# Expert layer of a two-layer decoder: inner values made transposed, gates repeated over the partitions through DRAM

## The reference

```
    def _L1_ffn_ref(x, W1, b1, W2, b2, Wr, br):
...
        logits = xf @ Wr + br
        _, topk_idx = jax.lax.top_k(logits, K)
        mask = jnp.zeros_like(logits).at[jnp.arange(T)[:, None], topk_idx].set(1.0)
        gates = mask + logits - jax.lax.stop_gradient(logits)
        h = jax.nn.relu(jnp.einsum('td,edh->eth', xf, W1) + b1[:, None, :])
        combined = jnp.einsum('te,eth,ehd->td', gates, h, W2) + gates @ b2
        return x + combined.reshape(B, S, D)
...
    x = x + _L1_ffn_ref(_layernorm(x, axis=-1), L1_ffn_W1, L1_ffn_b1, L1_ffn_W2, L1_ffn_b2, L1_ffn_Wr, L1_ffn_br)
```

## Time and profile before

| | us |
|---|---|
| median of three runs | 4103.48 (4102.7 to 4106.04) |
| profiled execution, its span | 4103.4 |
| PE busy | 3856.4 (94%) |
| DVE busy | 3013.6 (73%) |
| ACT busy | 2823.1 (69%) |
| POOL busy | 1820.6 (44%) |
| stage `experts`, first to last instruction on VectorE | 3744.09 to 4100.55 |

### The profile page before, as it was taken

One profiled execution on the slowest core, in us unless ns is written; L12 is line 12 of the kernel. 1 busy time (PEld: TensorE's weight loads), 2 busy tenths in 40 slices (PEclk: granted clock), 3 DMA queues, 4 the chain that ended last, 5 costly groups with the idle time before them and its releaser, 6 DMA issues. The chain is left out here.

```text
span 4103.4 us, 106549 instructions
## 1 busy us (share of the span) xinstructions
PE 3856.4 (94%) x33992; PEld 2993.1 (73%) x33992; DVE 3013.6 (73%) x7587; ACT 2823.1 (69%) x6420; POOL 1820.6 (44%) x1728
## 2 busy tenths in 40 slices
PE   7888899999979999898999989999999989998999
PEld 5666688888746666685666677888888867776777
DVE  7888655555569999657999955777777767775665
ACT  5666455555569999757999975777777767774333
POOL 3333222222258888536777753333333321112443
PEclk9999999999999999999999999999999989999999
DMA  0000100000010000100000010000000000000000
GB/s 18 9 9 10 48 8 6 6 6 6 7 43 9 8 8 8 27 18 10 8 8 8 13 28 29 1 0 0 0 0 0 0 3 4 3 3 6 12 12 12
DMA packets 109259, 42.48 MB, mean 10 GB/s; under 512 B 91232, under 2 KB 107872, under 8 KB 108512
## 3 DMA queue, kind: packets, MB, share of 16 engines
q1 hardware_dynamic: 109152, 41.10, 3.9%
HBM read 20.16 MB, written 4.19 MB: 6 GB/s over the span
## 5 line engine op out<-in xcount | busy, mean ns | idle before, releaser
L1142 POOL TENSOR_TENSOR l_rc<-l_rc,l_rs 128x1024 f32<-128x1024 f32 x128 | 303.6, 2372 | 201.4 <-DVE l_rs L1334 201.4
L1209 ACT ACTIVATE l_prob<-l_prob,l_mx 128x128 f32<-128x128 f32 x1024 | 312.1, 390 | 0.0
L1820 POOL TENSOR_TENSOR mb_steps<-w_upto,mb_dta 128x1024 f32<-128x1024 f32 x64 | 121.4, 1896 | 354.7 <-DVE mb_dta L2077 354.7
L711 POOL TENSOR_TENSOR ca_prob<-ca_prob,ca_sm 128x1232 f32<-128x1232 f32 x64 | 143.9, 2249 | 299.3 <-DVE ca_sm L877 299.3
L1234 PE MATMUL l_qk_ps<-w_local,l_hT 128*128 128x512 f32 x512 | 248.8, 609 | 13.1 <-DVE l_rs L1334 11.1
L1136 POOL TENSOR_TENSOR l_prob<-l_prob,l_sm 128x1024 f32<-128x1024 f32 x128 | 242.8, 1897 | 16.9 <-DVE l_sm L1320 16.9
L1119 POOL TENSOR_TENSOR l_rc<-l_rc,l_ss 128x1024 f32<-128x1024 f32 x128 | 243.4, 1902 | 12.5 <-POOL l_rc L1142 4.5
L1977 PE MATMUL mb_x_ps<-w_wx,mb_xT 128*128 128x256 f32 x1024 | 236.9, 384 | 0.0
L1329 DVE TENSOR_REDUCE l_ss<-l_sq 128x16 f32<-128x1024 f32 x128 | 156.1, 1219 | 77.3 <-ACT l_sq L1173 76.9
L2542 POOL TENSOR_TENSOR mo_hid<-mo_hid,mo_gate 128x1024 f32<-128x1024 f32 x64 | 121.7, 1901 | 201.7 <-DVE mo_hid L2688 201.7
L1977 PEld LDWEIGHTS mb_x_ps<-w_wx,mb_xT 128*128 128x128 f32 x1024 | 190.0, 191 | 23.2
(11 more groups left out here) (354 smaller groups left out, 11993.2 us busy)
## 6 DMA issues: line engine op xcount, KB each, us to landing
la_xin<-in_x SPq DMA_DIRECT2D x64, 64.0 KB
l_h<-lt_y SPq DMA_DIRECT2D x128, 32.0 KB
lt_quad<-lt_y SPq DMA_DIRECT2D x32, 128.0 KB
out_x<-k_x SPq DMA_DIRECT2D x64, 64.0 KB, 1.5
l_h<-lt_y SPq DMA_DIRECT2D x128, 31.8 KB
lt_quad<-lt_y SPq DMA_DIRECT2D x32, 127.0 KB
ca_ctxT<-in_ctx_T SPq DMA_DIRECT2D x128, 19.2 KB
wr_state<-in_p_state SPq DMA_DIRECT2D x1, 2438.5 KB, 11.9
```

The lines of the kernel that those rows point to most:

```text
L1142: gp.tensor_tensor(wide(rc[l][:]), wide(rc[l][:]), wide(rs[l][:]), ALU.add).then_inc(*pool_sum.did("rot"))
L1209: ex = sc.activation(p[:, a, j], p[:, a, j], ACT.Exp, bias=mx[l][:, a, j:j + 1])
```

## The change

The inner values are made with the inner index on the partitions, not the tokens. `w1` is held and `xnT` moves: eight products of 128 columns, piece j with the inner values of the experts 2j and 2j+1, partitions 0 to 63 the first and 64 to 127 the second. The eight turns of `hid` go. The bias now is one column for each piece (`b1`, 8 columns for 1024), so ScalarE adds it and applies the relu as it takes the values out of PSUM, in eight instructions of 128 columns; VectorE's add goes. `hid_ps` now has two lanes, `hidT` and `gateT` have four buffers.

The gates must then be repeated over the partitions. ScalarE's turned gates `gateT` (16 rows of 128) are stored by SP to `parked` in DRAM; SP waits for the landing and loads them back twice, the even experts' rows for partitions 0 to 63, the odd ones' for 64 to 127, each row read for 64 partitions, into `spread`. POOL multiplies `hidT` by `spread`. The bias product with `b2` moves behind the eight others. There are six parts, `NORM, TURN, ROUTE, GATE, SPREAD, OUT`: POOL multiplies batch n-4, PE's second product takes batch n-5, and VectorE's add and SP's store are for that batch too. The loop body has four steps.

```diff
-    "experts": (("w1", 1024), ("w2", 1024), ("b2", 128), ("wr", 16), ("b1", 1024), ("br", 16)),
+    "experts": (("w1", 1024), ("w2", 1024), ("b2", 128), ("wr", 16), ("b1", 8), ("br", 16)),
...
-        w1 = part["w1"].rearrange("p (e h) -> p e h", e=E)
+        w1 = part["w1"].rearrange("p (j n) -> p j n", j=CH)
...
+        hidT = [m.sb(f"hidT{i}", [128, CH, T]) for i in range(4)]
+        gateT = [m.sb(f"gateT{i}", [E, T]) for i in range(4)]
+        spread = both(m, "spread", [128, CH, T])
+        hid_ps = m.ps("hid_ps", [128, 2, CH, T])
...
             @block.sync
             def _(sp):
                 def step(at):
-                    b = at(LAST)
+                    b = at(GATE)
+                    if b:
+                        sp.wait_ge(*act_gate.at("gT", b))
+                        sp.dma_start(g.parked[b.lane], gateT[b.slot][:]).then_inc(parked[b.lane], 16)
+                        sp.wait_ge(parked[b.lane], b.loaded())
+                        for a in (0, 1):
+                            src = g.parked[b.lane].rearrange("(j a) t -> a j t", a=2)[a].partition_broadcast(64)
+                            sp.dma_start(spread[b.lane][64 * a:64 * a + 64], src).then_inc(spread_in[b.lane], 16)
+                    b = at(OUT)
                     if b:
...
             @block.gpsimd
...
-                    b = at(ROUTE)
-                    if b:
-                        l = b.lane
-                        gp.wait_ge(*vec_hid.at("hb", b))
-                        gp.tensor_tensor(hid[l][:], hid[l][:], gate[l][:].unsqueeze(2).to_broadcast([T, E, HID]), ALU.mult
-                                         ).then_inc(*pool_hid.did("hid"))
+                    b = at(SPREAD)
+                    if b:
+                        hid = hidT[b.slot][:]
+                        gp.wait_ge(*act_hid.at("h1", b))
+                        gp.wait_ge(spread_in[b.lane], b.loaded(32))
+                        gp.tensor_tensor(hid, hid, spread[b.lane][:], ALU.mult).then_inc(*pool_hid.did("hid"))
...
             @block.scalar
...
+                    b = at(TURN)
+                    if b:
+                        sc.wait_ge(*pe_turn.at("xnT", b))
+                        sc.wait_ge(*pe_route.at("h1", b, ago=2))
+                        sc.activation(xnT[b.lane][:], xn_ps[:, 0:T], ACT.Copy).then_inc(*act_turn.did("xnT"))
+                    b = at(GATE)
+                    if b:
+                        sc.wait_ge(*pe_gate.at("gT", b))
+                        sc.wait_ge(*pe_out.at("y", b, ago=4))
+                        sc.wait_ge(*pool_hid.at("hid", b, ago=2))
+                        sc.activation(gateT[b.slot][:], gate_ps[0:E, 0:T], ACT.Copy).then_inc(*act_gate.did("gT"))
                     b = at(NORM)
...
+                    b = at(ROUTE)
+                    if b:
                         for u in (0, 1):
-                            sc.wait_ge(*pe_out.at(f"hT{u}", b))
-                            sc.activation(hidT[l][:, 4 * u:4 * u + 4].rearrange("p j t -> p (j t)"),
-                                          turn_ps[:, 4 * u:4 * u + 4].rearrange("p j t -> p (j t)"), ACT.Relu
-                                          ).then_inc(*act_out.did(f"hT{u}"))
-                    b = at(TURN)
-                    if b:
-                        sc.wait_ge(*pe_turn.at("xnT", b))
-                        sc.activation(xnT[b.lane][:], xn_ps[:, 0:T], ACT.Copy).then_inc(*act_turn.did("xnT"))
-                pipeline(sc, g.NB, LAST + 1, step)
+                            sc.wait_ge(*pe_route.at(f"h{u}", b))
+                            sc.wait_ge(*pe_out.at("y", b, ago=4))
+                            for j in range(4 * u, 4 * u + 4):
+                                ex = sc.activation(hidT[b.slot][:, j], hid_ps[:, b.lane, j], ACT.Relu, bias=b1[:, j:j + 1])
+                            ex.then_inc(*act_hid.did(f"h{u}"))
...
             @block.tensor
...
-                    b = at(OUT)
-                    if b:
-                        l = b.lane
-                        te.wait_ge(*vec_route.at("gate", b))
-                        te.wait_ge(*act_out.at("hT1", b, ago=1))
-                        te.transpose(gate_ps[0:E, 0:T], gate[l][:], g.ident[:]).then_inc(*pe_out.did("gT"))
...
+                    b = at(GATE)
+                    if b:
+                        te.wait_ge(*vec_route.at("gate", b))
+                        te.wait_ge(*act_gate.at("gT", b, ago=1))
+                        te.transpose(gate_ps[0:E, 0:T], gate[b.lane][:], g.ident[:]).then_inc(*pe_gate.did("gT"))
+                    b = at(OUT)
+                    if b:
+                        te.wait_ge(*pool_hid.at("hid", b))
+                        te.wait_ge(*vec_out.at("x", b, ago=1))
+                        for j in range(CH):
+                            te.matmul(y_ps[:, 0:C], hidT[b.slot][:, j], w2[:, j], start=(j == 0), stop=False)
+                        te.matmul(y_ps[:, 0:C], gateT[b.slot][:], b2, start=False, stop=True).then_inc(*pe_out.did("y"))
...
-                        te.wait_ge(*vec_hid.at("hb", b, ago=1))
-                        for a in (0, 1):
-                            mm = te.matmul(hid_ps[:, a], xnT[l][:], w1[:, 8 * a:8 * a + 8].rearrange("p e h -> p (e h)"),
-                                           start=True, stop=True)
-                        mm.then_inc(*pe_route.did("h"))
-                    b = at(OUT)
-                    if b:
-                        l = b.lane
-                        te.wait_ge(*pool_hid.at("hid", b))
+                        te.wait_ge(*act_hid.at("h1", b, ago=2))
                         for u in (0, 1):
                             for j in range(4 * u, 4 * u + 4):
-                                mm = te.transpose(turn_ps[:, j], hid[l][:, 2 * j:2 * j + 2].rearrange("p e h -> p (e h)"),
-                                                  g.ident[:])
-                            mm.then_inc(*pe_out.did(f"hT{u}"))
-                        te.wait_ge(*act_out.at("gT", b))
-                        te.wait_ge(*vec_out.at("x", b, ago=1))
-                        te.matmul(y_ps[:, 0:C], gateT[l][:], b2, start=True, stop=False)
-                        for j in range(CH):
-                            if j % 4 == 0:
-                                te.wait_ge(*act_out.at(f"hT{j // 4}", b))
-                            mm = te.matmul(y_ps[:, 0:C], hidT[l][:, j], w2[:, j], start=False, stop=(j == CH - 1))
-                        mm.then_inc(*pe_out.did("y"))
-
-                pipeline(te, g.NB, LAST + 1, step)
+                                mm = te.matmul(hid_ps[:, l, j], w1[:, j], xnT[l][:], start=True, stop=True)
+                            mm.then_inc(*pe_route.did(f"h{u}"))
...
             @block.vector
...
-                        v.wait_ge(*vec_route.at("gate", b))
-                        v.wait_ge(*pe_route.at("h", b))
-                        v.wait_ge(*pe_out.at("hT1", b, ago=2))
-                        v.tensor_tensor(hid[l][:].rearrange("p e h -> p (e h)"), hid_ps[:].rearrange("p a n -> p (a n)"), b1,
-                                        ALU.add).then_inc(*vec_hid.did("hb"))
...
+    dram["parked"] = nc.dram_tensor("parked", [2, 16, T], F32, kind="Internal").ap()
```

42 lines of the change are left out of this document (20 added, 22 removed).

## The result

| | before | after |
|---|---|---|
| median (lowest to highest), us | 4103.73 (4102.58 to 4107.67) | 4115.85 (4114.2 to 4118.42) |
| ratio, 95% interval | | 1.0029 (1.0020 to 1.0038) |
| span of the profiled execution | 4103.4 | 4114.0 |

The change makes the kernel slower by 0.3%; I had forecast 1.0% faster. The steady steps gained nothing: between VectorE's 11th and 57th add to the stream a batch takes 5.43 us in both kernels. What is lost stands at the stage's ends. The first add is at 3763.98 instead of 3760.19 us, the ten steps behind it take 4.0 us more, the last seven 2.7 more, and the last add is at 4110.81 instead of 4100.26.

What follows compares the result with a forecast made beforehand. PE was taken to bound the `experts` stage, its step falling from 5.43 to 4.72 us. Start 3747.8 + fill 15 + 60 x 4.72 = 283.2 + drain 13.1 + end 2.85 gave 4062 us, range 4050 to 4096.

Steps and rivals of the forecast that it cites:

- PE's own step: PE's work per batch in the last stage, `experts`: falls from 5.43 to 4.72 us, saving 0.71.
- ScalarE: Eight evacuations with bias take 2.44 us, at most 3.08; ScalarE's 3.5 to 4.1 a batch is no bound by itself.
- VectorE: VectorE loses its add over 1024 values; it waits for PE anyway, so nothing is gained directly.
- Rival C: Gates reach PE's gate turn late: no stall or 0.1 us a batch, 4062 to 4068; within the main forecast's 0.60.
- The trip: Gates' way on SP's queue: store to DRAM, landing, two loads of 512 KB in all, POOL's wake; 4.6 to 5.3 us.
- D: Length of the gates' trip, from ScalarE's gate copy to POOL's wake: 4.6 to 5.3 us.
- packets much more than 27 ns: Sign named for being wrong first: the loads' 512-byte packets taking much longer than the 27 ns assumed.
- Round (1): Loop over three steps through PE, ScalarE, the trip and POOL: 13.3 to 14.0 us, hidden within 14.16.
- Rival A: Trip only half hides through slower data, landing or evacuations: step 4.85 to 5.3 us, 4070 to 4097; chance 0.20.
- Rival B: SP's queue sets the step: at the small load's 109 GB/s, step 6.7 us, time 4181; chance 0.13.
- round (2): SP's queue in order, loads' data, output store, next gate store, landing, wake: 3.6 to 4.3 us, under PE's 4.72.
- Sum: Forecast total time of the changed kernel: 4062 us, 41 us or 1.0% faster.

Runs made afterwards that it cites:

- e8: Changed kernel without POOL's product, the store of the gates and both loads; PE waits for ScalarE's evacuations instead: 4074.45 us, ratio 0.9932.
- e1: Changed kernel with VectorE's copy of the two largest values replaced by a reduction over an axis of one: 4104.06 us, ratio 1.0003.
- e5: Changed kernel with POOL's product reading one column of `spread` repeated instead of all of it: 4107.42 us, ratio 1.0012.
- e3: Changed kernel with loads reading an input's rows and waiting for POOL alone; store kept behind them, with SP's wait for it: 4126.74 us, ratio 1.0061.
- e14: e12 with PE's turn of `xn` also moved behind the second product, and ScalarE's copy of it: 4085.19 us, ratio 0.9957.
- e12: e6 with PE's gate turn behind the second product and ScalarE's gate copy behind its logarithm and exponential: 4083.81 us, ratio 0.9950.
- e13: Changed kernel with loads reading an input's rows and waiting for POOL alone, and no store of the gates: 4087.46 us, ratio 0.9963.
- e6: Changed kernel with one more step between gates and product (product n-5, second product n-6, four `spread` buffers): 4085.41 us, ratio 0.9952.

## Why the prediction was wrong

**PE's own step: right.** 4.72 forecast, 4.68 measured in e8. That is close in part by luck: the first product takes 1.87 in place of 1.98 and the second 1.94, while the gap behind the routing product is 0.1 wider.

**ScalarE: right, and cheaper.** Eight evacuations in a row start 0.25 us apart (383 ns each, overlapping), 2.2 us for all, against my 2.44.

**VectorE: the step that failed.** "It waits for PE anyway; nothing is gained directly" is true of the add that goes, and I stopped there. I looked at what VectorE waits for by semaphore, and at no other tie. In the kernel before POOL's product began right behind the gates of its own batch and VectorE's add, and was over before the next batch's copy: 0.17 us, 50 copies of 50. The change frees it from that place: when it runs is set by the trip. Nothing in the earlier trace rows shows the price of a copy beside a product, and the prediction does not name this as an unmeasured thing. The round that it closes costs 5.43 - 5.02 = 0.41 us a batch, 60 x 0.41 = 25 us. Taking the copy alone out of it gave 0.18 back (e1), since `xn` waits in its place.

**Rival C was true and too cheap.** I had 1.99 + 0.05 us from routing to the gates; e8 shows 2.40. The logits start 0.43 behind the start of routing (0.26 forecast), and L2689 takes 0.35 instead of 0.17. It reads two tiles of SBUF while POOL adds `xn` to the stream, and ends 0.03 us behind that add 50 times of 50: one more tie of VectorE to POOL. Coming late costs 0.3 a batch, some 18 us, against the 0 to 6 forecast.

**The trip: every term in its place, three too small.** D = 0.02 + 1.35 + 4.72 = 6.1 us, against 4.6 to 5.3. The store's part, 1.36, and the first byte of the loads, 1.35, were met. The data took 2.6 (1.7 to 2.4 forecast), the landing with wake 0.7 (0.35). The sign "packets much more than 27 ns" did not come: in the burst from 3888.5 to 3891.5 us the 1152 packets of 512 bytes take 27 ns in the median, 31 in the mean. The product took 2.35, the price of L1142 which I had named as the dear end and not taken; the full second operand costs what it costs there, as e5's 1.91 confirms.

The estimate from the Trainium skill ("DMA: Bandwidth & Descriptors", Anatomy of one DMA), 5.7 us, was nearer to D than my sum, but by luck. The store's part took 1.36 us and not 2.0, the loads' part 4.72 and not the 3.7 that 2.0 + 1.7 gives. The page has that figure for DMAs that GpSimd issues, and that it speaks against two dependent transfers was my conclusion from the figure. The Trainium skill ("SBUF — State Buffer", Door 1: The DMA port swizzle) gave an estimate of 2.4 us for the data, close to the 2.6 measured with `out_x` among them. Its 218 GB/s as a cap is less sure: in the two slices before the second load's first bytes, issued 0.63 us behind the first, 238 and 303 GB/s are shown, too short a stretch to decide.

**Round (1): "it hides" failed too, but did not set the time.** With the measured evacuations, product and trip it is 8.7 - 0.3 + 0.45 + 6.1 = 15.0, over the 14.16 of three steps. That is 5.0 a step, no more than PE takes in e8 anyway. The round that bound goes over two, with nothing but the gates, the trip and the product in it. It is closed by a link that is in no semaphore.

**Rival A** (PE idle through a trip that half hides) gave the size of the trip's excess but named POOL as the engine that PE waits for; PE waited for VectorE. **Rival B** did not come in the changed kernel, but round (2) did in e3 and e14, and SP was as full in e12. It came not through bytes: a small store behind a large load, waited for in order.

**Sum.** 4062 + 18 (gates late) + 25 (the copy's round) = 4105. The remaining 11 stand in filling and draining, by the adds shown at the top. e13 and e6, with the steady step of e8, carry 5 to 7 over 4062 + 18. How the rest is shared between the longer trip, the lower clock from 3760 on and copies that wait in the first steps was not separated.

## What to carry to other kernels

When an engine's work is moved to another time, ask what it will stand beside, not only whom it waits for. Here a GpSimd operation of 2.35 us held a VectorE copy, a `tensor_scalar` or an SBUF-only `tensor_tensor` until it ended, even a copy of two values; put these where they have slack, or read one operand from PSUM. A trip through DRAM costs some 6 us here and wants whole steps of pipeline between; and a small transfer that somebody waits for doesn't belong in order behind large ones on the same queue.

## What the hardware showed that I had not expected

- VectorE's 128x2 copy took 0.17 to 2.32 us beside POOL's product and ended 0.02 to 0.05 us behind it in all 275 cases counted; a reduction of the same two values took 0.155 us.
- VectorE's last operation on the gates, 128x16 with both inputs in SBUF, took 0.35 to 0.38 us in the changed kernel, beside POOL's add of 128x128, and ended 0.03 us behind it, 50 times of 50; without such an add, in the kernel before, it took 0.17 to 0.18.
- POOL's 128x1024 product took 2.35 us with two full operands and 1.91 with a repeated one.
- A store of 8 KB let the loads out 1.35 us after its issue on an idle queue, 2.9 with `out_x` between 512 KB of loads and itself. Right behind the loads it landed after 3.6 to 3.8.
- A load whose pattern starts with a dimension of size 2 ran at 50 GB/s, where two loads of 64 partitions each made 220 together.
- PE's work for a batch fell by 0.16 us (4.68 to 4.52) when the turns stood between the bias product and the routing; the start from routing to the first product fell from 0.24 to 0.14.
